# Slot filling behind the first pair's weights, and fewer waits in TensorE's program for sorted tiles

## Chip, cores and metric

The kernel runs on one core of a Trainium2 chip, as one launch. The metric is the time of that launch on the device in microseconds (us), the median of several runs. The core has five engines that run programs of their own and meet at semaphores: TensorE (PE; the profile lists its matmuls as PE and its weight loads as PEld), VectorE (DVE), ScalarE (ACT), GpSimd (POOL) and SyncE (SP). Of each engine the instructions that only wait, load a register or issue a DMA are shown as its own queue (PEq or PEldq, DVEq, SPq and so on) and don't count as busy.

## The reference

Input x is 16 sequences of 256 tokens, 128 wide, in float32: 4096 tokens. Eight sublayers follow one another, each added to x behind a layer norm. A lookahead attention with 16 heads, a mixture of 8 experts of which the best 2 serve each token, a latent attention, and the same mixture again make layer 0; a helical attention, a mixture of which the best 1 serves each token, a recurrent (delta) attention, and that mixture again make layer 1.

```python
x = x + attn_a0(layernorm(x), W_qkv, W_out)        # aa
x = x + top2(layernorm(x), Wg, bg, W1, b1, ...)    # fa
x = x + attn_b0(layernorm(x), ...)                 # ab
x = x + top2(layernorm(x), Wg, bg, W1, b1, ...)    # fb
x = x + attn_a1(layernorm(x), ...)                 # helical
x = x + top1(layernorm(x), gate_w, ...)            # fc
x = x + attn_b1(layernorm(x), ...)                 # delta
x = x + top1(layernorm(x), gate_w, ...)            # fd
# top2, of one token x and its two experts e with weights w_e:
#   y = x + sum_e w_e * (relu(x @ W1[e] + b1[e]) @ W2[e] + b2[e]), then a layer norm with gamma and beta
# top1, of one token and its expert: shared(x) + (silu(x' @ gate[e].T) * (x' @ up[e].T)) @ down[e].T,
#   with x' = x * sigmoid(largest logit)
```

## The kernel before

The stages run one behind the other, each between barriers of all engines. x, its normed form and constants stay in SBUF. The two parts that the change touches are these.

**The start of the lookahead attention** (stage aa, from L264). It takes 8 pairs of heads, and for each the 16 sequences, 128 steps. SP's program (L303 to L316) begins with four DMAs that have nothing to do with attention: they fill four DRAM buffers, into which the mixtures will sort their tokens, from a tile of zeros and default addresses in SBUF (`rt_empty`, made by POOL in the stage before at L155 and L160): two `rt_pairs` (L306) and two `rt_slots` (L308). Behind them comes a loop over the pairs, its first turn written out with the integer 0 (`turns`, L57): wait until the pair before was projected (L312; `reached` leaves a wait for 0 out, L34), ask for the pair's weights `aa_w` (L313), wait, ask for its output weights (L315). At the end (L316) SP waits for all four fillings. POOL copies each step's input (L335), PE projects it (`project`, L363 and L367; L360 waits for the weights), ACT keeps the projections (L471), and the other engines follow. A layer norm (L242, L260) runs ahead of the stage.

**The sorted tiles of the four mixtures.** A mixture sends every token's row by an indirect DMA to a slot, so that the tokens of one expert lie in whole tiles of 128 slots; slots that are left over keep the filling. Then it loads the slots in parts, each with its own semaphore `arrived[i]`, and works through the tiles, whose expert is read from a small table `owner`. In `top2_mixture` (fa and fb, L842) there are 71 tiles, in parts that begin at tiles 0, 4 and 20; in `routed_mixture` (fc and fd, L1185) 39, in parts that begin at 0, 4 and 16. Each tile j takes these steps; all buffers between engines are double, `yout` fourfold:

- PE turns the tile (`turn_x`, L994; L1314), ACT keeps it as `xT` (`keep_x`).
- PE projects it with its expert's weights (`up`, L1000; `both`, L1318 to L1323). The expert's number is first read into a register (`value_load`, L997; L1317).
- In fa and fb DVE adds the bias (L1135), giving `hid` and `bias_ok`. In fc and fd ACT makes a tanh, and DVE two steps (L1468 and L1472), giving `hid` and `rhid_ok`.
- PE turns `hid` (`turn_h`, L1007; L1330), ACT keeps it as `hidT` (L1061: relu; L1383) and signals `h_ok`.
- PE projects it down (`lower`, L1016; L1339), DVE writes `yout` (`keep_y`, L1142; L1479) once the return of four tiles before has landed and signals `y_ok`; POOL returns it by an indirect DMA to the tokens' rows (L941; L1261). At the start of a part POOL first converts the part's addresses (`home`, L937).

PE's program is unrolled and skewed; a turn n holds

```python
turn_x(n); turn_h(n - 3); lower(n - 4); up(n - 1)      # both(n - 1) in fc and fd
```

and each of these steps waits with two `wait_ge`: for its input, and (through `reached`) for the reader of the buffer that it writes again, two tiles back. Of two waits in front of one instruction the compiler attaches one to the instruction and issues the other as an instruction of its own, which the trace lists as EVENT_SEMAPHORE at L37, the line of `reached`.

Of the kernel before, what the change touches and what calls it, by code (L numbers as in the profile page):

```python
# [18 lines left out]
P = 128  # L19
# [14 lines left out]
def reached(eng, sem, count):  # L34

    if not isinstance(count, int) or count > 0:
        eng.wait_ge(sem, count)  # L37
# [19 lines left out]
def turns(eng, count):  # L57

    yield 0
    with eng.Fori(1, count) as i:  # L60
        yield i
# [202 lines left out]
def lookahead_attention(nc, sh, rt, empty, W_qkv, W_out):  # L264
# [8 lines left out]
    with Phase(nc, "aa") as ph:  # L273
        emptied = ph.sem("emptied")
# [27 lines left out]
        with nc.Block() as block:  # L302
            @block.sync  # L303
            def _(sp):
                for slots in rt.slots2:
                    sp.dma_start(slots.rearrange("(j p) c -> p j c", p=P), empty[:]).then_inc(emptied, 16)  # L306
                for slots in rt.slots:
                    sp.dma_start(slots.rearrange("(j p) c -> p j c", p=P), empty[:, 0:rt.tiles, 0:rt.ROW]  # L308
                                 ).then_inc(emptied, 16)
                for p in turns(sp, PAIRS):  # L310

                    reached(sp, projected, 3 * BATCH * p)  # L312
                    sp.dma_start(w[:], w_dram[:, :, bass.ds(p * P, P)]).then_inc(w_in, 16)  # L313
                    reached(sp, y_mm, BATCH * p)
                    sp.dma_start(wo[:], W_out[bass.ds(p * P, P), :]).then_inc(wo_in, 16)  # L315
                sp.wait_ge(emptied, 64)  # L316

            @block.gpsimd
# [523 lines left out]
def top2_mixture(nc, sh, rt, slots, name, Wg, bg, W1, b1, W2, b2, gamma, beta):  # L842
# [8 lines left out]
    PARTS = ((0, 4), (4, 20), (20, ROUTED))  # L851
    with Phase(nc, name) as ph:
# [31 lines left out]
        arrived = [ph.sem(f"arrived{i}") for i in range(len(PARTS))]  # L884
# [7 lines left out]
        def part_of(j):  # L892
            return next(i for i, (lo, hi) in enumerate(PARTS) if lo <= j < hi)

        with nc.Block() as block:
# [55 lines left out]
            def _(pe):  # L951
# [37 lines left out]
                owners = {}  # L989

                def turn_x(j):
                    pe.wait_ge(arrived[part_of(j)], 16)
                    reached(pe, x_ok, j - 1)
                    nc.tensor.transpose(ps_t[:, j % 2, 0:P], xin[:, j, 2:P + 2], sh.ident[:]).then_inc(x_mm, 1)  # L994

                def up(j):
                    owners[j] = nc.tensor.value_load(owner[0:1, j:j + 1], min_val=0, max_val=E - 1)  # L997
                    pe.wait_ge(x_ok, j + 1)
                    reached(pe, bias_ok, j - 1)
                    nc.tensor.matmul(ps_up[:, j % 2, 0:F], xT[:, j % 2, :],  # L1000
                                     w1[:, bass.ds(owners[j], 1), :].rearrange("p a c -> p (a c)"),
                                     start=True, stop=True).then_inc(up_mm, 1)

                def turn_h(j):
                    pe.wait_ge(bias_ok, j + 1)
                    reached(pe, h_ok, j - 1)
                    for i in range(2):  # L1007
                        ins = nc.tensor.transpose(ps_h[:, j % 2, i * P:(i + 1) * P], hid[:, j % 2, i * P:(i + 1) * P],
                                                  sh.ident[:])
                    ins.then_inc(h_mm, 1)  # L1010
# [14 lines left out]
                for n in range(ROUTED + 4):  # L1025
                    if n < ROUTED:
                        turn_x(n)
                    if 0 <= n - 3 < ROUTED:
                        turn_h(n - 3)
                    if 0 <= n - 4 < ROUTED:  # L1030
                        lower(n - 4)
                    if 0 <= n - 1 < ROUTED:
                        up(n - 1)
# [151 lines left out]
def routed_mixture(nc, sh, ew, rt, slots, name, gate_w):  # L1185
# [9 lines left out]
    PARTS = ((0, 4), (4, 16), (16, ROUTED))  # L1195
    with Phase(nc, name) as ph:
# [27 lines left out]
        arrived = [ph.sem(f"arrived{i}") for i in range(len(PARTS))]  # L1224
        fetched = [ph.sem(f"fetched{i}") for i in range(4)]

        def part_of(j):
            return next(i for i, (lo, hi) in enumerate(PARTS) if lo <= j < hi)

        with nc.Block() as block:  # L1230
# [35 lines left out]
            def _(pe):  # L1266
# [42 lines left out]
                owners = {}  # L1309

                def turn_x(j):
                    pe.wait_ge(arrived[part_of(j)], 16)
                    reached(pe, x_ok, j - 1)
                    nc.tensor.transpose(ps_t[:, j % 2, 0:P], xin[:, j, 1:P + 1], sh.ident[:]).then_inc(x_mm, 1)  # L1314

                def both(j):
                    owners[j] = nc.tensor.value_load(owner[0:1, j:j + 1], min_val=0, max_val=E - 1)  # L1317
                    pe.wait_ge(x_ok, j + 1)  # L1318
                    reached(pe, rhid_ok, j - 1)
                    nc.tensor.matmul(ps_g[:, j % 2, 0:F], xT[:, j % 2, :],  # L1320
                                     ew.gate[:, bass.ds(2 * owners[j], 2), :].rearrange("p a c -> p (a c)"),
                                     start=True, stop=True)
                    nc.tensor.matmul(ps_g[:, j % 2, F:2 * F], xT[:, j % 2, :],  # L1323
                                     ew.up[:, bass.ds(2 * owners[j], 2), :].rearrange("p a c -> p (a c)"),
                                     start=True, stop=True).then_inc(both_mm, 1)

                def turn_h(j):
                    pe.wait_ge(rhid_ok, j + 1)
                    reached(pe, h_ok, j - 1)
                    for i in range(2):  # L1330
                        ins = nc.tensor.transpose(ps_u[:, j % 2, i * P:(i + 1) * P], hid[:, j % 2, 0, i * P:(i + 1) * P],  # L1331
                                                  sh.ident[:])
                    ins.then_inc(h_mm, 1)
# [14 lines left out]
                for n in range(ROUTED + 4):  # L1348
                    if n < ROUTED:
                        turn_x(n)  # L1350
                    if 0 <= n - 3 < ROUTED:
                        turn_h(n - 3)
                    if 0 <= n - 4 < ROUTED:
                        lower(n - 4)
                    if 0 <= n - 1 < ROUTED:
                        both(n - 1)
# [1017 lines left out]
```

## Time and profile before

| | |
|---|---|
| median of 3 runs | 4413.18 us (4410.03 to 4414.11) |
| profiled execution | 4403.01 us, of which the span of instructions 4401.3 us |
| PE busy | 3398.4 us (77%), its weight loads 2798.6 us (64%) |
| DVE busy | 2698.6 us (61%) |
| ACT busy | 1907.2 us (43%) |
| POOL busy | 1609.0 us (37%) |
| mean granted clock of PE | 0.881 |

The median is the number that a change is compared with; the profiled execution is one run whose every instruction was recorded, and the durations of single steps come from it. Shares of busy time are means over stages with different limits, so they say little of a single stage. The core's 16 DMA engines move 96.03 MB in all.

### The profile page before, as it was taken

How to read it: one execution, taken by the hardware profiler on the slowest of the kernel's cores; microseconds unless marked ns; L12 is line 12 of the kernel's file. 1: busy time of each engine (PE TensorE's matmuls, PEld its weight loads, DVE VectorE, ACT ScalarE, POOL GpSimd, SP SyncE). 2: the span in 40 equal slices, each digit the busy share in tenths (PEclk: the TensorE clock that was granted, in tenths of full speed). 3: DMA queues.
4: the chain of work that ended last, by engine and by line, in shares of the span. 5: the costliest groups of instructions: out<-in, count | busy, mean ns of one | idle time of the engine just before them, and what ended most of it. 6: DMA issues, size and time to landing. Idle time of an engine off the chain costs nothing. (4 is left out here: it accounts for less than half of the span.)

```text
span 4401.3 us, 91493 instructions
## 1 busy us (share of the span) xinstructions
PE 3398.4 (77%) x23484; PEld 2798.6 (64%) x23484; DVE 2698.6 (61%) x8449; ACT 1907.2 (43%) x5752; POOL 1609.0 (37%) x2825
## 2 busy tenths in 40 slices
PE   0999999999994649999983838999999685433176
PEld 0888888888883536777763616888888563322155
DVE  2566666666663365666661444777777255999954
ACT  0555555555551215555541324666666233211122
POOL 1222222222223734444435622333333051666633
PEclk6999999999995869999995969999999697766578
DMA  9000000000001220000002210000000121000003
GB/s 154 3 4 4 0 4 4 4 1 4 4 0 53 86 58 8 2 4 3 2 3 65 84 49 5 6 6 6 6 6 6 33 59 29 1 1 1 1 18 88
DMA packets 137483, 96.03 MB, mean 22 GB/s; under 512 B 21552, under 2 KB 127296, under 8 KB 137088
## 3 DMA queue, kind: packets, MB, share of 16 engines
q1 hardware_dynamic: 124160, 67.30, 6.9%
q0 software_dynamic: 13184, 27.19, 1.8%
q8 instruction: 49, 0.80, 0.1%
q14 instruction: 90, 0.74, 0.1%
HBM read 45.86 MB, written 43.87 MB: 20 GB/s over the span
## 5 line engine op out<-in xcount | busy, mean ns | idle before, releaser
L340 POOL TENSOR_TENSOR aa_prob<-aa_prob,aa_inv 128x128 f32<-128x128 f32 (+1 forms) x512 | 249.2, 508 | 991.5 <-DVE aa_inv L556 991.5
L363 PE MATMUL aa_proj<-aa_xs,aa_w 128*128 128x256 f32 x1280 | 362.3, 398 | 86.4 <-DMA aa_w<-in_L_attn_a_W_qkv 85.0
L471 ACT ACTIVATE aa_qkv<-aa_proj 128x512 f32<-128x512 f32 x384 | 229.4, 597 | 331.4 <-PE aa_proj L363 270.7
L650 POOL TENSOR_TENSOR ab_prob<-ab_prob,ab_inv 128x128 f32<-128x128 f32 (+1 forms) x512 | 248.8, 507 | 334.2 <-DVE ab_inv L805 327.5
L773 ACT ACTIVATE ab_prob<-ab_ps_score,ab_low 128x128 f32<-128x128 f32 (+1 forms) x512 | 211.7, 424 | 303.5 <-PE ab_ps_turn L707 301.5
L1845 ACT ACTIVATE lm_prob<-lm_ps_score,lm_low 128x256 f32<-128x256 f32 x512 | 237.7, 470 | 234.8 <-DVE lm_low L1914 160.5
L1790 PEld LDWEIGHTS lm_ps_out<-la_v,lm_probT 128*128 128x128 f32 x2048 | 253.3, 191 | 72.4 <-issue 66.1
L1732 POOL TENSOR_TENSOR lm_sq<-lm_comp 128x512 f32<-128x512 f32 x128 | 133.7, 1044 | 441.2 <-DVE lm_comp L1887 441.2
L363 PEld LDWEIGHTS aa_proj<-aa_xs,aa_w 128*128 128x128 f32 x1280 | 213.8, 191 | 118.8 <-issue 86.5
L529 DVE SCALAR_TENSOR_TENSOR aa_look<-aa_th_look,aa_ahead 128x384 f32<-128x384 f32 x256 | 183.2, 716 | 161.9 <-ACT aa_th_look L477 161.9
L2174 PE MATMUL dr_bank<-da_rT,da_spread 128*128 (+1 forms) x256 | 95.8, 462 | 240.6 <-ACT dr_RW L2192 232.9
L1769 PE MATMUL lm_ps_score<-lm_unit 128*128 128x256 f32 x1024 | 270.5, 387 | 5.5 <-DVE lm_unit L1904 5.5
L1790 PE MATMUL lm_ps_out<-la_v,lm_probT 128*128 (+1 forms) x2048 | 257.2, 252 | 19.0 <-issue 13.3
L2224 POOL TENSOR_TENSOR dr_toward<-dr_S,XN 128x64 f32<-128x64 f32 x512 | 180.8, 372 | 212.8 <-DVE dr_S L2253 150.5
L260 PE MATMUL n_turned<-ident,XN 128*128 128x128 f32 x256 | 55.6, 370 | 234.3 <-DVE XN L242 234.1
L799 DVE TENSOR_REDUCE ab_low<-ab_ps_score 128x1 f32<-128x128 f32 (+1 forms) x512 | 147.1, 349 | 141.3 <-PE ab_ps_score L700 141.3
L1914 DVE TENSOR_REDUCE lm_low<-lm_ps_score 128x2 f32<-128x512 f32 x256 | 176.4, 689 | 92.9 <-PE lm_ps_score L1769 90.9
L482 ACT ACTIVATE aa_th_su<-aa_look_su 128x384 f32<-128x384 f32 x256 | 125.7, 491 | 242.8 <-PE aa_look_su L407 242.8
L488 ACT ACTIVATE aa_prob<-aa_minus,aa_low 128x128 f32<-128x128 f32 (+1 forms) x512 | 225.4, 444 | 0.9 <-DVE aa_low L548 0.9
L2174 PEld LDWEIGHTS dr_bank<-da_rT,da_spread 128*128 128x128 f32 x256 | 58.7, 236 | 255.6 <-issue 245.9
L536 DVE SCALAR_TENSOR_TENSOR aa_gated<-aa_th_su,aa_look_su 128x384 f32<-128x384 f32 x256 | 141.8, 554 | 108.3 <-ACT aa_th_su L482 106.7
L1904 DVE TENSOR_TENSOR lm_unit<-lm_comp,lm_inv_n 64x512 f32<-64x512 f32 x256 | 201.4, 787 | 1.9 <-ACT lm_inv_n L1834 0.2
(507 smaller groups left out, 9960.3 us busy)
## 6 DMA issues: line engine op xcount, KB each, us to landing
rt_pairs<-rt_empty SPq DMA_DIRECT2D x2, 4615.0 KB, 36.4
rt_slots<-rt_empty SPq DMA_DIRECT2D x2, 2515.5 KB, 39.7
fa_xin<-rt_back SPq DMA_DIRECT2D x8, 512.0 KB, 7.3
fb_xin<-rt_back SPq DMA_DIRECT2D x8, 512.0 KB, 7.3
lm_unit<-la_qk SPq DMA_DIRECT2D x256, 16.0 KB
XN<-rt_back SPq DMA_DIRECT2D x8, 512.0 KB, 5.7
fa_xin<-rt_pairs SPq DMA_DIRECT2D x1, 3315.0 KB
fb_xin<-rt_pairs SPq DMA_DIRECT2D x1, 3315.0 KB
```

The lines of the kernel that those rows point to most:

```text
L340: ins = nc.gpsimd.tensor_tensor(prob[:, h, a:b], prob[:, h, a:b], inv[:, h, t:t + 1].broadcast_to([P, b - a]), ALU.mult)
L363: ins = nc.tensor.matmul(proj[:, i * SEQ:(i + 1) * SEQ], w[:, m, :], xs[:, k, :], start=True, stop=True)
L471: nc.scalar.activation(qkv[:, k, j, :, :].rearrange("p a b -> p (a b)"), proj[:], ACT.Copy, scale=SCALE if j == 0 else 1.0).then_inc(kept, 1)
L488: nc.scalar.activation(prob[:, h, a:b], minus[:, h, a:b], ACT.Exp, bias=low[:, h, t:t + 1], scale=-1.0, accum_out=total[:, h, t:t + 1]).th ...
L529: nc.vector.scalar_tensor_tensor(out=look[:, h, :], in0=th_look[:, h, :], scalar=1.0, in1=ahead[:], op0=ALU.add, op1=ALU.mult).then_inc(lo ...
L650: ins = nc.gpsimd.tensor_tensor(prob[:, h, a:b], prob[:, h, a:b], inv[:, h, t:t + 1].broadcast_to([P, b - a]), ALU.mult)
L773: nc.scalar.activation(prob[:, h, a:b], ps_score[:, h, a:b], ACT.Exp, bias=low[:, h, t:t + 1], accum_out=total[:, h, t:t + 1]).then_inc(ex ...
L1769: ins = nc.tensor.matmul(ps_score[:, h, c * SEQ:(c + 1) * SEQ], unit[:, j, i, h, 0, c, :], unit[:, j, i, h, 1, :, :], start=True, stop=True)
L1790: ins = nc.tensor.matmul(ps_out[:, i, (2 * h + s) * HD:(2 * h + s + 1) * HD], probT[:, h, t, s * P:(s + 1) * P], v[:, bass.ds((n % BATCH) ...
L1845: nc.scalar.activation(prob[:, h, s, :], ps_score[:, h, s * SEQ:(s + 1) * SEQ], ACT.Exp, bias=low[:, h, s:s + 1], accum_out=totals[:, i, h ...
L1904: ins = nc.vector.tensor_tensor(unit[rows, j, i, h], comp[rows, j, i], inv_n[rows, j, i].unsqueeze(2).broadcast_to([64, 2, 2, HALF]), ALU. ...
L2224: nc.gpsimd.tensor_tensor(toward[:, :, part], S[:, :, part], WV[:, half, :, part, j], ALU.add).then_inc(toward_ok, 1)
```

## The change

In the first turn of SP's loop the four fillings are issued behind the request for the pair's weights and its output weights, no longer in front of them. In the sorted tiles of all four mixtures PE's program loses waits: `turn_x` waits for `arrived` in the first tile of a part alone, and the `reached` waits of `turn_x`, `up` (or `both`) and `turn_h` are gone. Each of the events that they waited for is implied by another wait that PE's program has already passed: `up(n - 1)` waits for `x_ok` of tile n - 1, so `turn_x(n + 1)` needn't; `turn_h(j - 2)` stands in front of `up(j)` and waits for `bias_ok` (or `rhid_ok`) of tile j - 2; `lower(j - 2)` stands in front of `turn_h(j)` and waits for `h_ok`. The waits of `lower` are kept. Nothing else changes.

```diff
--- before.py
+++ after.py
@@ -302,17 +302,18 @@
         with nc.Block() as block:
             @block.sync
             def _(sp):
-                for slots in rt.slots2:
-                    sp.dma_start(slots.rearrange("(j p) c -> p j c", p=P), empty[:]).then_inc(emptied, 16)
-                for slots in rt.slots:
-                    sp.dma_start(slots.rearrange("(j p) c -> p j c", p=P), empty[:, 0:rt.tiles, 0:rt.ROW]
-                                 ).then_inc(emptied, 16)
                 for p in turns(sp, PAIRS):
 
                     reached(sp, projected, 3 * BATCH * p)
                     sp.dma_start(w[:], w_dram[:, :, bass.ds(p * P, P)]).then_inc(w_in, 16)
                     reached(sp, y_mm, BATCH * p)
                     sp.dma_start(wo[:], W_out[bass.ds(p * P, P), :]).then_inc(wo_in, 16)
+                    if isinstance(p, int):
+                        for slots in rt.slots2:
+                            sp.dma_start(slots.rearrange("(j p) c -> p j c", p=P), empty[:]).then_inc(emptied, 16)
+                        for slots in rt.slots:
+                            sp.dma_start(slots.rearrange("(j p) c -> p j c", p=P), empty[:, 0:rt.tiles, 0:rt.ROW]
+                                         ).then_inc(emptied, 16)
                 sp.wait_ge(emptied, 64)
 
             @block.gpsimd
@@ -989,21 +990,19 @@
                 owners = {}
 
                 def turn_x(j):
-                    pe.wait_ge(arrived[part_of(j)], 16)
-                    reached(pe, x_ok, j - 1)
+                    if j == PARTS[part_of(j)][0]:
+                        pe.wait_ge(arrived[part_of(j)], 16)
                     nc.tensor.transpose(ps_t[:, j % 2, 0:P], xin[:, j, 2:P + 2], sh.ident[:]).then_inc(x_mm, 1)
 
                 def up(j):
                     owners[j] = nc.tensor.value_load(owner[0:1, j:j + 1], min_val=0, max_val=E - 1)
                     pe.wait_ge(x_ok, j + 1)
-                    reached(pe, bias_ok, j - 1)
                     nc.tensor.matmul(ps_up[:, j % 2, 0:F], xT[:, j % 2, :],
                                      w1[:, bass.ds(owners[j], 1), :].rearrange("p a c -> p (a c)"),
                                      start=True, stop=True).then_inc(up_mm, 1)
 
                 def turn_h(j):
                     pe.wait_ge(bias_ok, j + 1)
-                    reached(pe, h_ok, j - 1)
                     for i in range(2):
                         ins = nc.tensor.transpose(ps_h[:, j % 2, i * P:(i + 1) * P], hid[:, j % 2, i * P:(i + 1) * P],
                                                   sh.ident[:])
@@ -1309,14 +1308,13 @@
                 owners = {}
 
                 def turn_x(j):
-                    pe.wait_ge(arrived[part_of(j)], 16)
-                    reached(pe, x_ok, j - 1)
+                    if j == PARTS[part_of(j)][0]:
+                        pe.wait_ge(arrived[part_of(j)], 16)
                     nc.tensor.transpose(ps_t[:, j % 2, 0:P], xin[:, j, 1:P + 1], sh.ident[:]).then_inc(x_mm, 1)
 
                 def both(j):
                     owners[j] = nc.tensor.value_load(owner[0:1, j:j + 1], min_val=0, max_val=E - 1)
                     pe.wait_ge(x_ok, j + 1)
-                    reached(pe, rhid_ok, j - 1)
                     nc.tensor.matmul(ps_g[:, j % 2, 0:F], xT[:, j % 2, :],
                                      ew.gate[:, bass.ds(2 * owners[j], 2), :].rearrange("p a c -> p (a c)"),
                                      start=True, stop=True)
@@ -1326,7 +1324,6 @@
 
                 def turn_h(j):
                     pe.wait_ge(rhid_ok, j + 1)
-                    reached(pe, h_ok, j - 1)
                     for i in range(2):
                         ins = nc.tensor.transpose(ps_u[:, j % 2, i * P:(i + 1) * P], hid[:, j % 2, 0, i * P:(i + 1) * P],
                                                   sh.ident[:])
```

## Rows read from the trace of the kernel before

**Rows 1.** Windows: length, PE, PEld, DVE, ACT, POOL busy, clock, DMA share, GB/s

```profile
0.00:110.00 110.00, 6.84 (x32) 4.65 (x32) 25.62 (x75) 6.30 (x10) 15.12 (x32) 0.67 0.91 154
110.00:1320.00 1210.00, 1182.80 (x9194) 1017.19 (x9194) 792.50 (x2555) 710.57 (x2046) 290.58 (x636) 0.99 0.01 3
```

**Rows 2.** List of waits, 0 to 140 us: who <- whom: total, times, longest

```profile
PE aa_proj L363 <- DMA aa_w<-in_L_attn_a_W_qkv: 78.7, 1, 78.7
```

**Rows 3.** Timeline, 0 to 140 us: start, duration, instruction [idle before <- for what]

```profile
35.08 18.18 SPq L306 DMA_DIRECT2D rt_pairs<-rt_empty  x2
...
91.08 13.89 SPq L313 DMA_DIRECT2D aa_w<-in_L_attn_a_W_qkv  x1
...
112.44 2.05 PE L363 MATMUL aa_proj<-aa_xs,aa_w 128*128 128x256 f32 x4 [78.69 <-DMA aa_w<-in_L_attn_a_W_qkv]
```

**Rows 4.** Timeline of sorted tiles in fa, around 1484 and 1511 us

```profile
1484.87 0.97 POOL L941 DMA_INDIRECT rt_back<-fa_yout,fa_home  x1 [0.30 <-issue]
...
1511.29 0.30 PEld L1000 LDWEIGHTS fa_ps_up<-fa_w,fa_xT 128*128 128x128 f32 x2 [0.22 <-issue]
...
1512.35 0.38 ACT L1061 ACTIVATE fa_hidT<-fa_ps_h 128x256 f32<-128x256 f32 x1
...
1512.77 0.30 PEld L1000 LDWEIGHTS fa_ps_up<-fa_w,fa_xT 128*128 128x128 f32 x2 [0.20 <-issue]
```

**Rows 5.** PE's queue by line: count: ns min/median/max, first to last start

```profile
L37 PEldq EVENT_SEMAPHORE  x3: 51/51/51, 1511.3 to 1511.6; - x3
...
L997 PEldq SEQ_ASSERT  x1: 18/18/18, 1512.5 to 1512.5; - x1
...
L1000 PEldq FUSED_REGOPS  x1: 46/46/46, 1512.7 to 1512.7; - x1
...
L997 PEldq SEQ_ASSERT  x1: 18/18/18, 2432.9 to 2432.9; - x1
...
L1000 PEldq FUSED_REGOPS  x1: 52/52/52, 2433.0 to 2433.0; - x1
...
L37 PEldq EVENT_SEMAPHORE  x1: 51/51/51, 3602.2 to 3602.2; - x1
```

**Rows 6.** Timeline of fc around 3600 us and fd around 4307 us

```profile
3599.71 0.69 PE L1320 MATMUL fc_ps_g<-gateT,fc_xT 128*128 x2
...
3601.75 0.42 DVE L1472 SCALAR_TENSOR_TENSOR fc_hid<-fc_gu,fc_ps_g 128x256 f32<-128x256 f32 x1
...
3603.42 0.30 PEld L1320 LDWEIGHTS fc_ps_g<-gateT,fc_xT 128*128 128x128 f32 x2
...
4306.66 0.30 PEld L1320 LDWEIGHTS fd_ps_g<-gateT,fd_xT 128*128 128x128 f32 x2 [0.43 <-issue]
...
4308.30 0.30 PEld L1320 LDWEIGHTS fd_ps_g<-gateT,fd_xT 128*128 128x128 f32 x2
```

**Rows 7.** Timeline, 256 to 268 us: the second pair's weights

```profile
258.31 0.61 SPq L313 DMA_DIRECT2D aa_w<-in_L_attn_a_W_qkv  x1
...
262.23 1.13 PE L363 MATMUL aa_proj<-aa_xs,aa_w 128*128 128x256 f32 x4 [1.14 <-DMA aa_w<-in_L_attn_a_W_qkv]
```

**Rows 8.** Short windows, columns as in rows 1

```profile
38.00:40.00 2.00, 0.00 (x0) 0.00 (x0) 0.00 (x0) 0.00 (x0) 0.06 (x1) 0.50 1.14 266
112.00:120.00 8.00, 6.19 (x16) 4.01 (x16) 0.00 (x0) 1.20 (x2) 0.00 (x0) 0.50 0.00 0
1472.00:1480.00 8.00, 7.83 (x50) 6.26 (x49) 3.51 (x10) 3.53 (x12) 4.82 (x7) 1.00 1.20 303
```

**Rows 9.** By line, 1472 to 1480 us: count | busy, mean ns | idle

```profile
L1061 ACT ACTIVATE fa_hidT<-fa_ps_h 128x256 f32<-128x256 f32 x6 | 2.3, 384 | 0.0
```

**Rows 10.** POOL's returns by line, in fa (from tile 4) and fb

```profile
L941 POOL DMA_INDIRECT rt_back<-fa_yout,fa_home x66: 966/969/985, 1481.0 to 1578.2; - x66
...
DMA to landing us min/median/max: 2.3/2.3/3.2
...
L941 POOL DMA_INDIRECT rt_back<-fb_yout,fb_home x71: 966/969/1001, 2438.4 to 2544.4; - x71
```

## The prediction

> **What bounds the kernel now.** I began with the busy times by stretch, the page's slices and then windows: TensorE (PE) is busy for 1182.8 of the 1210 us from 110 to 1320, but for 6.8 of the first 110 [rows 1]. The change touches that stretch and the four sorted mixtures, so each was then read by itself.
>
> In the first 140 us the list of waits has one entry that matters: the projection waits 78.7 us for the DMA that brings its weights [rows 2]. The timeline says why. The stage opens at 35.08 with SyncE (SP) issuing the four slot fillings; the instruction that asks for the weights comes up only at 91.08, takes 13.89 us to issue behind them, and the first matmul starts at 112.44 [rows 3]. Nothing computes meanwhile, and the fillings have no reader before the first mixture, beyond 1350 us.
>
> In the sorted tiles PE looks full, but its weight loads show an idle piece in front of the first projection of every tile, put down to "issue" [rows 4]: nothing the profile shows was waited for. The cause is found by asking for the lines of PE's own queue, whose instructions are not counted as busy. Per tile it loads the owner, works out addresses, asserts, and executes four stand-alone waits, before it can issue [rows 5]. The steps of PE from tile to tile (1511.29 to 1512.77, 1.48 us [rows 4]) are the length of that list. The other two mixtures (fc, fd) are read from [rows 6]: there steps of two lengths alternate, which points to a loop over two tiles.
>
> **Part 1, the fillings behind the first weights.** Moved past are four DMA issues, all on SP's queue; GpSimd's (POOL) queue holds no DMA in this stage. The weights are then asked for at 35.08. How long they take alone is shown by the second pair: asked for at 258.31, its first matmul waits for them until 262.23, 3.92 us [rows 7]. So the first matmul comes at 39.00 instead of 112.44: **73.4 us**. In 38 to 40 the granted clock is at its lower level, as it is in 112 to 120 [rows 8], so the cold start of the stage is only moved, not saved.
>
> What the fillings now run beside: issue 56.0 us (35.08 to 91.08) and data until just before 112.44, some 76 us, so from about 37 to 114, next to the first ten steps of attention. Behind them on SP stands the second pair's request, now at 258.31 and then at about 185, with 70 us to spare; the stage's closing wait for them lies over a thousand us later. Does the traffic slow the engines? The nearest stretch is 1472 to 1480, where slots are loaded at 303 GB/s while all engines work [rows 8]: the ReLU activation takes 384 ns on the mean there [rows 9] and 0.38 us at 1512.35, when little moves [rows 4]. That is loading into SBUF and not reading from it, so it is only near. I take nothing; as far bound, a tenth of 76 us, 7.6 us lost. If the weights' packets were served in turn with the fillings' and not ahead of them, 3.92 us would at most double. Bounds of this part: 73.4 down to 73.4 - 7.6 - 3.9 = 61.9; better than 73.4 is excluded by the same 3.92 us.
>
> **Part 2, the waits of the 71-tile mixtures (fa, fb).** Three of four stand-alone waits per tile go; the attached wait for the arrival goes without an instruction of its own. A wait executes in 51 ns, but costs its dispatch too. With one between them, the assert and the address arithmetic start at 1512.5 and 1512.7; in the second tile of fb, where that wait does not exist yet, at 2432.9 and 2433.0 [rows 5]. Three waits with a turn in between start within 0.3 us, 1511.3 to 1511.6 [rows 5]. So 0.1 us each, between 0.05 (execution alone) and 0.12; three are 0.3, and PE's list falls from 1.48 to about 1.18 us a tile.
>
> It will not be followed that far, for another is late next: POOL, which returns each tile. Back to back a return takes 1.27 us, 0.97 busy and 0.30 of its own issue ahead of it (the one at 1484.87 [rows 4]), while from the fifth tile 65 steps take 97.2 us (1481.0 to 1578.2), 1.495 each [rows 10]. The forecast is that POOL sets the step: 66 steps x (1.495 - 1.27) = 14.9, less some 0.5 for the index cast of the third part, which is hidden now, and 0.3 for the first tiles: 14.1. The first four tiles keep their times, since their returns wait behind the slot loads. The second pass (71 returns, 2438.4 to 2544.4 [rows 10]) has the same pace: **28.2 us** for both. Bounds: with 0.05 us a wait, 0.15 x 132 = 19.8; not more than 29.8, all of POOL's slack.
>
> **Part 3, the waits of the 39-tile mixtures (fc, fd).** Same three waits, but the list is not what binds. One tile's first projection starts at 3599.71, its hidden layer ends on VectorE (DVE) at 3601.75 + 0.42 = 3602.17, PE's queue executes its next stand-alone wait at 3602.2 [rows 5], and the projection two tiles on is loaded at 3603.42 [rows 6]. So PE's queue stands at the turning of the hidden layer, whose weight load carries the wait for DVE, until DVE is done, and the loop of 3.71 us over two tiles is: 2.46 to the hidden layer and 1.25 of queue. Of the removed waits only the one before the projection lies in the 1.25; the other two are executed while the queue would stand anyway, and their cover is that standing. Gain 0.1 per two tiles, 0.05 x 76 = **3.8 us** for both; bounds 0 and, were the loop gone, PE's shortest step of 1.64 (4306.66 to 4308.30 [rows 6]) against 1.855: 0.215 x 76 = 16.3.
>
> For this the Trainium skill has a rule that says otherwise (Perfetto Trace Analysis, section Tensor Engine Instruction): a matrix instruction with a semaphore wait is pushed into a wait queue and the sequencer goes on to the next instruction. By the rule in the Trainium skill the queue would not stand, this part would be at its upper bound of 16.3 instead of 3.8, and the sum 117.9. The record at 3602.2, just behind DVE's end, speaks against it.
>
> **The sum.** 73.4 + 28.2 + 3.8 = 105.4. The profiled execution took 4403.0 us (span 4401.3), 10 us under the median of the runs, 4413.2; the difference is carried to the median: 4413.2 - 105.4 = **4307.8** (4297.6 by the profiled execution's own time).
>
> **Rivals.**
> *PE does not stand at attached waits.* If PE's queue goes on past a weight load whose wait is still open, the loop over two tiles is gone: fc and fd fall to 1.64 a tile, 16.3 instead of 3.8, time 4295.3. For it: some steps already take 1.64. Against it: the alternation and the place of the stand-alone wait [rows 5, 6]. 6%. (This is what the rule of the Trainium skill, Perfetto Trace Analysis, would make of these stages.)
>
> *The tiles stay where they are.* DVE keeps a tile's output only when the return of four tiles before has landed. Landing takes 2.3 us [rows 10]; with steps of 1.27, four take 5.1, which leaves over a microsecond. If returns landed as late as they do under the slot loads, or another loop held PE, parts 2 and 3 would give nothing: 4413.2 - 73.4 = 4339.8. 6%.
>
> *The fillings press on the attention stage.* The 7.6 and 3.9 us above are lost: 4319.3. For it: it is 76 us of 16 busy DMA engines reading the memory that the engines read. Against it: the means of [rows 9]. 11%.
>
> *Slower than before.* Place: the second pair's weights, behind the fillings on SP's queue. If the fillings, now beside work, ran on past 185, PE would stand for each microsecond more, as it does today. To give back all 105.4 they would have to end near 290 rather than 114, three times as long; at the 7.6 us allowed above they are far from it. At four times, some 340, the time would be 4413 + 50 = 4463. 1%.
>
> The forecast itself holds the other 76%.
>
> **How the numbers follow.** Low end: all upper bounds, 73.4 + 29.8 + 16.3 = 119.5, 4293.7, taken as 4294, which holds the first rival. High end: all lower bounds, 61.9 + 19.8 + 0 = 81.7, 4331.5, taken as 4331, which holds the third. Left out are the second and fourth rivals and a rest. A measurement of this kernel can tell about 0.2% (8.8 us) from no change. Every case but the fourth gains over 70 us: faster 0.98, same 0.01, slower 0.01.
>
> **What would show it right or wrong.** Right: the first matmul of the projection near 39 us; a wait for the weights near 5 us in place of 78.7; the fillings' data beside attention until about 114, and the second pair's weights unharmed; in fa and fb, POOL's returns 1.27 us apart through most of the pass, their idle time put down to "issue" and no longer to DVE; PE's stand-alone waits down from four to one a tile; in fc and fd, pairs of steps that sum to some 3.6 us, with the one stand-alone wait still right behind DVE's hidden layer. Wrong: attention steps longer before 114 than after (then the third rival), returns still 1.5 apart with PE idle (the second), or fc at 1.64 (the first).

## The result, and the profile after

The changed kernel takes **4297.98 us** in the median of 4 runs (4294.72 to 4310.06) against 4411.99 before (4 runs): 114.0 us less, a ratio of 0.9746 with a 95% interval of 0.9726 to 0.9767. Forecast were 4307.8 us and a gain of 105.4, with 4294 to 4331 as the range. Run again beside the experiments below, it took 4296.67 us (5 runs) against 4406.64 (9 runs), 0.9761 [0.9745, 0.9776]: 110.0 us less. The recorded execution took 4310.06 us (span 4308.3), 92.9 under the recorded one of before. That the same change shows 93, 110 and 114 us is itself a part of what had to be explained.

**The start of the attention.** The timeline of the changed kernel from 30 to 140 us (start, duration, instruction, idle before it) answers to [rows 3]:

```profile
35.08 0.61 SPq L308 DMA_DIRECT2D aa_w<-in_L_attn_a_W_qkv  x1
...
36.42 23.50 SPq L313 DMA_DIRECT2D rt_pairs<-rt_empty  x2
...
39.54 2.05 PE L364 MATMUL aa_proj<-aa_xs,aa_w 128*128 128x256 f32 x4 [5.79 <-DMA aa_w<-in_L_attn_a_W_qkv]
...
59.96 45.25 SPq L315 DMA_DIRECT2D rt_slots<-rt_empty  x2
```

The weights are asked for first, and the projection starts at 39.54 instead of 112.44; the wait is 5.79 us where it was 78.69. SP needs 69 us to issue the fillings (56 before), beside a working attention.

**The sorted tiles.** POOL's returns from the fifth tile on, of fa and then of fb (count: ns min/median/max, first to last start; below each, what ended the idle time ahead of them, in us and times), answer to [rows 10]:

```profile
L942 POOL DMA_INDIRECT rt_back<-fa_yout,fa_home x67: 964/971/982, 1409.0 to 1497.5; - x67
...
  DVE fa_yout L1141: 18.9, 43
  issue: 7.0, 23
...
L942 POOL DMA_INDIRECT rt_back<-fb_yout,fb_home x67: 964/969/985, 2365.1 to 2452.9; - x67
...
  DVE fb_yout L1141: 16.7, 38
  issue: 8.5, 28
```

66 steps take 88.5 us in fa and 87.8 in fb, 1.34 and 1.33 each, where they took 1.495. The forecast was 1.27. And in 43 of 67 cases in fa, 38 in fb, POOL still waits for DVE: it isn't the one that sets the step.

In fc one tile of the changed kernel reads, in the timeline (and, the third row, in the lines of PE's own queue, as in [rows 5]):

```profile
3512.35 0.42 DVE L1469 SCALAR_TENSOR_TENSOR fc_hid<-fc_gu,fc_ps_g 128x256 f32<-128x256 f32 x1
...
3513.98 0.30 PEld L1318 LDWEIGHTS fc_ps_g<-gateT,fc_xT 128*128 128x128 f32 x2 [0.17 <-issue]
...
L37 PEldq EVENT_SEMAPHORE  x1: 51/51/51, 3512.8 to 3512.8; - x1
```

The hidden layer ends at 3512.77, PE's queue executes its next stand-alone wait at 3512.8, and the projection is loaded at 3513.98: 1.21 us behind the hidden layer, where [rows 6] give 1.25. Over the tiles 6 to 34 the mean fell from 1.263 to 1.180 (0.083), the median from 1.258 to 1.161 (0.097) and the least from 1.254 to 1.149 (0.105). A stand-alone wait in this list takes 0.051 us and the pause that comes with it 0.055, so the least shows the whole of one wait; in some tiles a longer pause elsewhere in the list takes a part back.

By stage (from the first to the last instruction that writes one of the stage's own tiles; the sixth line from the helical stage's last matmul to the first transpose of the expert weights; us):

| | before | changed | changed, again |
|---|---|---|---|
| attention aa | 1292.4 | 1219.3 | 1219.0 |
| fa | 258.9 | 250.2 | 247.2 |
| fb | 259.8 | 248.7 | 247.7 |
| fc | 155.6 | 153.0 | 153.1 |
| fd | 155.3 | 154.0 | 153.9 |
| projection behind the helical attention | 37.0 | 39.2 | 30.3 |
| span | 4401.3 | 4308.3 | 4291.3 |

The first five lines give 96.9 and 101.0 us. The sixth has nothing to do with the change, and differs by 9 us between two recordings of one program.

### The profile page after: what moved, and what is told of

Its sections match the earlier page's. It is cut to its first block and busy times, and to the rows that moved or that the text cites. A ratio compares the mean times of both kernels' runs of the same rounds, so it can differ in the third digit from the quotient of the medians.

```text
span 4308.3 us, 90857 instructions
## 1 busy us (share of the span) xinstructions
PE 3387.3 (79%) x23484; PEld 2803.7 (65%) x23484; DVE 2698.0 (63%) x8449; ACT 1907.7 (44%) x5752; POOL 1608.3 (37%) x2825
## 5 line engine op out<-in xcount | busy, mean ns | idle before, releaser
L1787 PEld LDWEIGHTS lm_ps_out<-la_v,lm_probT 128*128 128x128 f32 x2048 | 254.0, 192 | 72.6 <-issue 66.1
L1911 DVE TENSOR_REDUCE lm_low<-lm_ps_score 128x2 f32<-128x512 f32 x256 | 176.6, 690 | 92.3 <-PE lm_ps_score L1766 90.3
```

The source lines that it names most:

```text
L1787: ins = nc.tensor.matmul(ps_out[:, i, (2 * h + s) * HD:(2 * h + s + 1) * HD], probT[:, h, t, s * P:(s + 1) * P], v[:, bass.ds((n % BATCH) ...
```

## The experiments

**1. The fillings alone.** The first hunk of the change, and nothing of the others.

> Part 1 alone: the slot fillings issued behind the first pair's weights, every wait of the sorted tiles kept. Theory: the attention stage (first to last instruction 1292.4 us before, 1219.3 in the changed kernel) takes 1219 to 1220, the sorted stages keep their lengths of before (first to last projection of the tiles: fa 106.7, fb 107.7, fc 71.5, fd 72.5), and the whole is 73 us faster than the kernel before, some 4338 us. Rival (the fillings press on the attention, and the changed kernel's waits hid that): attention over 1225 us. Rival (the fillings only move the loss): total within 20 us of before.

It took 4328.09 us, the kernel before beside it 4414.84. In the timeline of this kernel:

```profile
39.01 2.04 PE L364 MATMUL aa_proj<-aa_xs,aa_w 128*128 128x256 f32 x4 [5.29 <-DMA aa_w<-in_L_attn_a_W_qkv]
```

The attention took 1218.3 us. From its first projection to its end it takes 1214.3 us here, 1214.9 in the changed kernel and 1215.1 in the kernel before, so the fillings cost the work beside them nothing that can be seen. The sorted stages kept their lengths only roughly: from first to last projection fa and fb took 109.4 and 109.3 us, 2.6 and 1.5 more than in the recording of before, with the same code; fc took 71.6 and fd 71.5. The median step from projection to projection in fa and fb is 1.51 us as before, and the longer steps lie around the tenth tile; sums over a whole stage can differ by this much without any change. Between the recordings the gain is 74.9 us (4401.3 and 4326.4), against the run beside it 87, larger than 73; the next two experiments say why it can be.

**2. The waits alone.** All hunks but the first.

> Parts 2 and 3 alone: waits left out in all four mixtures, the fillings in front of the first weights as before. Theory: the attention stage takes 1292 us as before; from first to last projection fa 97.7, fb 96.6, fc 70.1, fd 70.4 us as in the changed kernel, each within 1 us; the whole 20 to 25 us faster than before. Rival (the two parts help each other, since the difference of the medians, 114 us, is more than 73 + 24): fa and fb shorter still than in the changed kernel, or the whole more than 30 us faster.

It took 4377.81 us, 37.0 less than before. The sorted stages were as in the changed kernel (97.4, 95.5, 70.0 and 70.1 us from first to last projection), but the attention took 1303.3 us and not 1292:

```profile
123.44 2.05 PE L363 MATMUL aa_proj<-aa_xs,aa_w 128*128 128x256 f32 x4 [89.72 <-DMA aa_w<-in_L_attn_a_W_qkv]
```

The first projection came 11 us later than in [rows 3], with the same instructions ahead of it. So the price of the fillings in front is no constant. Against the recording of before the four sorted stages together took 28.3 us less and the projection behind the helical attention 6.6 (30.4 against 37.0), the attention 10.9 more: 24.0 of the 25.3 us between the spans (4401.3 and 4376.0). The run of the kernel before beside this one was 37.0 us slower, over the 30 that the rival named; that would follow if its first projection, too, came near 123, but it was not recorded. Parts 1 and 2 don't help each other: fa and fb are no shorter than in the changed kernel by more than its own two recordings differ.

**3. The kernel before, recorded again.**

> The kernel before, recorded once more, for the spread. In its first recorded execution the first projection started at 112.4 us and the whole took 4403.0, 10 us under the median; in the run with the waits alone it started at 123.4. Theory: what differs between executions of the kernel before is how long the fillings take, so that the first projection starts between 112 and 124 us here, the attention stage from there to its end takes 1215 us as in every run so far, and an execution of 4411 to 4415 us goes with a start near 122. Rival (the spread lies elsewhere, in PE's clock in the later stages): a start near 112 and a total above 4410, or the reverse.

```profile
114.57 2.05 PE L363 MATMUL aa_proj<-aa_xs,aa_w 128*128 128x256 f32 x4 [80.83 <-DMA aa_w<-in_L_attn_a_W_qkv]
```

4404.26 us, with a first projection at 114.57 and 1215.4 us from there to the attention's end. Three recordings with the fillings in front thus give 112.4, 114.6 and 123.4; those without, here and below, 38.8 to 39.7. Neither recording of the kernel before was one of 4411 to 4415 us, so that those go with a start near 122 stays unproven.

The record names the chip of each of these runs, and the length of the fillings goes with it. Experiments 1, 2, 5 and 6 ran on one chip: in each of their four recordings 115 to 165 GB/s still move between 118 and 122 us. This one and experiments 4 and 7 ran on a second, experiment 8 on a third: there it is at most 4 GB/s. The kernel before took 4414.84 us (one run) on the first, and in the median of nine runs 4406.64 on the second and 4399.83 on the third. So a part of what the fillings cost depends on the chip, as far as these recordings show; for the runs of the result the chip is not on record.

**4. Half of the fillings in front.** The changed kernel, with

```diff
+                for slots in rt.slots2:
+                    sp.dma_start(slots.rearrange("(j p) c -> p j c", p=P), empty[:]).then_inc(emptied, 16)
                 for p in turns(sp, PAIRS):
...
                     if isinstance(p, int):
-                        for slots in rt.slots2:
-                            sp.dma_start(slots.rearrange("(j p) c -> p j c", p=P), empty[:]).then_inc(emptied, 16)
                         for slots in rt.slots:
```

> The changed kernel with two of the four fillings (rt_pairs, 9.23 of 14.26 MB, 18 us of issue) put back in front of the first weights, the other two left behind them. Theory: the weights' packets stand behind the fillings' data, which moves at about 190 GB/s, so the first projection starts at 35 + 49 + 4 = 88 us, between 80 and 95. Rival (only SP's issue of the fillings counts, 18 to 24 us, and the data runs beside): at 57 to 63 us. The whole is later than the changed kernel by the same amount, since nothing else depends on it.

```profile
35.05 19.45 SPq L306 DMA_DIRECT2D rt_pairs<-rt_empty  x2
54.54 25.82 SPq L310 DMA_DIRECT2D aa_w<-in_L_attn_a_W_qkv  x1
...
87.78 2.05 PE L364 MATMUL aa_proj<-aa_xs,aa_w 128*128 128x256 f32 x4 [54.06 <-DMA aa_w<-in_L_attn_a_W_qkv]
```

The first projection starts at 87.78, forecast 88. So it is the data of the fillings that the weights stand behind, and not only their issue: SP is free for the weights at 54.5, and the instruction itself then takes 25.8 us to issue where it takes 0.6 with nothing in front. The whole took 4337.71 us, 41 more than the changed kernel's median beside it (4296.67), where 49 were expected; the attention alone is 47.9 us longer than in that kernel's recording (1266.9 and 1219.0), the span 44.6.

**5. The waits split by stage.** fa and fc lose only the wait in front of the projection, fb and fd only the others. The edit of `top2_mixture` (that of `routed_mixture` is the same with fc, `both` and `rhid_ok`):

```diff
+                alone = name == "fa"
...
-                    if j == PARTS[part_of(j)][0]:
+                    if alone or j == PARTS[part_of(j)][0]:
                         pe.wait_ge(arrived[part_of(j)], 16)
+                    if alone:
+                        reached(pe, x_ok, j - 1)
...
                     pe.wait_ge(x_ok, j + 1)
+                    if not alone:
+                        reached(pe, bias_ok, j - 1)
...
                     pe.wait_ge(bias_ok, j + 1)
+                    if alone:
+                        reached(pe, h_ok, j - 1)
```

> The changed kernel with its waits split by stage: fa and fc lose only the wait in front of the projection (up, both); fb and fd lose only the others (turn_x's two and turn_h's). Theory of the prediction: in fa and fb the length of PE's list binds, so each wait that goes is worth 0.1 us a tile: fa's middle steps 1.38 to 1.41, fb's 1.28 to 1.33. In fc and fd PE's queue stands at the turning of the hidden layer, so only the wait in front of the projection counts: fc 70.0 us from first to last projection as in the changed kernel, fd 72.5 as before. Rival (every executed wait counts alike): fc about 70.9, fd about 71.1. Rival (PE's queue never stands, a full gain was blocked by something else): fc and fd both as in the changed kernel.

The weight loads of the projections (two a tile; count: ns, first to last start) of this kernel:

```profile
L1330 PEld LDWEIGHTS fc_ps_g<-gateT,fc_xT x78: 186/189/337, 3495.1 to 3566.1; 128*128 128x128 f32 x78
L1330 PEld LDWEIGHTS fd_ps_g<-gateT,fd_xT x78: 186/189/337, 4218.4 to 4290.7; 128*128 128x128 f32 x78
L1005 PEld LDWEIGHTS fa_ps_up<-fa_w,fa_xT x142: 186/189/338, 1394.5 to 1497.2; 128*128 128x128 f32 x142
L1005 PEld LDWEIGHTS fb_ps_up<-fb_w,fb_xT x142: 186/189/338, 2357.6 to 2456.7; 128*128 128x128 f32 x142
```

By the same rows fa and fb take 106.8 and 107.8 us in the kernel before and 97.9 and 96.6 in the changed one (95.5 and 95.8 recorded again), fc and fd 71.6 and 72.6 before (71.6 and 71.5 in experiment 1) and 70.1 and 70.4 changed.

In fa and fb the stalls at the start of the parts blur these sums; the median step from one projection to the next leaves them out. It is 1.51 us in the kernel before, 1.42 with one wait gone (fa; 1.38 to 1.41 were expected), 1.37 with two (fb; 1.28 to 1.33 expected), and 1.31 and 1.32 with all three. So each wait was worth less than 0.1 us, and both stages missed their range. For fb the loop of the next experiment gives a reason: the wait that stays there stands in it, and 1.32 with a third of 0.105 is 1.36, an estimate; it was not tested by itself.

In fd (72.3) the two waits gave nothing that stands out of 71.5 to 72.6, where the rival that every wait counts alike had 71.1: they are executed while the queue stands. In fc the one wait gave 0.6 of 1.5 us, and its 71.0 is nearer to that rival's 70.9 than to the 70.0 expected; fd is what speaks against the rival. The trace shows where a part of the rest stayed: over the tiles 6 to 34 the pause in PE's queue in front of the address arithmetic of `lower`, behind the hidden layer, is 0.12 us in the median here and 0.08 in the changed kernel. What makes it is not settled.

**6. Owner loads ahead of a wait.** In the changed kernel the number of the tile's expert is loaded one place earlier: in fa on DVE in front of `keep_y`, in fb and fc on PE in front of `turn_h`; fd is left as it is. On PE (`owner_of` holds the `value_load` that stood in `up` and `both`):

```diff
                     if n < ROUTED:
                         turn_x(n)
+                    if name in ('fb', 'fc') and 0 <= n - 1 < ROUTED:
+                        owner_of(n - 1)
                     if 0 <= n - 3 < ROUTED:
                         turn_h(n - 3)
```

It tests what sets the 1.33 us. In the changed kernel's timeline of fa one loop over three tiles reads:

```profile
1443.42 0.30 PEld L1000 LDWEIGHTS fa_ps_up<-fa_w,fa_xT 128*128 128x128 f32 x2
...
1444.28 0.61 PE L1015 MATMUL fa_ps_y<-fa_w,fa_hidT 128*128 x4
...
1444.93 0.35 DVE L1141 TENSOR_SCALAR fa_yout<-fa_ps_y,fa_xin 128x128 f32<-128x128 f32 x1
...
1445.76 0.42 DVE L1134 TENSOR_TENSOR fa_hid<-fa_ps_up,fa_b1b 128x256 f32<-128x256 f32 x1 [0.48 <-PE fa_ps_h L1007]
...
1447.39 0.30 PEld L1000 LDWEIGHTS fa_ps_up<-fa_w,fa_xT 128*128 128x128 f32 x2
```

and in the lines of DVE's and PE's own queues, between them:

```profile
L1131 DVEq TENSOR_LOAD <-fa_owner x1: 306/306/306, 1444.9 to 1444.9; - x1
...
L37 PEldq EVENT_SEMAPHORE  x1: 51/51/51, 1446.2 to 1446.2; - x1
```

Behind the projection of 1443.42 PE comes to the next `lower`, which ends at 1444.89; `keep_y` follows at 1444.93; only with it does DVE's queue come to the owner load of the next bias, so the bias starts 0.83 us behind it, though its input is ready at 1445.43; it ends at 1446.19, PE's queue goes on at 1446.2 with its own owner load, and the next projection but two is loaded at 1447.39. 3.97 us over three tiles are 1.32 a tile.

> The changed kernel with an owner load moved ahead of a wait: in fa on DVE (ahead of keep_y), in fb and fc on PE (ahead of turn_h), fd untouched. Theory: the steps of 1.31 us that are left in fa and fb are a loop over three tiles: lower ends, keep_y starts, DVE's list (0.83 us to the bias), bias 0.43, PE's list (1.15 us to the projection), PE's own work 1.47 to the end of the next lower: 3.95 over three tiles. Shortening either list by 0.65 us takes the loop to 1.10, and POOL's 1.27 binds in fa and in fb alike: first to last projection 95 us in both (97.7 and 96.6 in the changed kernel), middle returns all at 1.27 to 1.29. In fc the loop over two tiles falls from 3.6 to 2.95 us, PE's own work of 1.63 a tile binds: 63 us instead of 70.1; fd stays at 70.4. Rival (POOL and late returns make the 1.31): fa and fb unchanged. Rival (PE's queue goes on past an attached wait): fc unchanged at 70.

The returns of this kernel in fa (DVE's load ahead) and fb (PE's), from the fifth tile on, and the projections of fc and fd:

```profile
L942 POOL DMA_INDIRECT rt_back<-fa_yout,fa_home x67: 963/967/982, 1408.4 to 1493.0; - x67
...
L942 POOL DMA_INDIRECT rt_back<-fb_yout,fb_home x67: 963/968/982, 2359.0 to 2443.2; - x67
...
L1337 PEld LDWEIGHTS fc_ps_g<-gateT,fc_xT x78: 190/192/337, 3476.7 to 3540.1; 128*128 128x128 f32 x78
L1337 PEld LDWEIGHTS fd_ps_g<-gateT,fd_xT x78: 186/189/338, 4190.6 to 4260.8; 128*128 128x128 f32 x78
```

66 steps take 84.6 and 84.2 us, 1.28 each, whichever of the two lists is shortened: now POOL's 1.27 binds, and "issue" ended its idle time 47 times of 67 in fa and 39 times in fb. fc fell to 63.4 us, every step but the first three and the last 1.64, the shortest that PE's own work had shown in [rows 6]; fd, untouched, stayed at 70.2. The passes themselves came to 91.9 and 90.9 us from first to last projection, 3 to 4 us under the expectation of 95, in part because that went by POOL's pace and forgot that PE may be further ahead of POOL at the end: in fb the last return starts 6.0 us behind the last projection, in the changed kernel 4.6.

**7. The loads ahead in all four mixtures,** on PE alone, and the changed kernel once more beside it.

> The changed kernel with PE's owner load put ahead of turn_h in all four mixtures. From the run that had it in fb and fc: fa and fb 91 us from first to last projection (97.7 and 96.6), POOL's returns 1.27 us apart throughout; fc and fd 63.3 us (70.1 and 70.4), every step 1.64. Together 26 us under the changed kernel, some 4270 us. Rival (the gain of one stage is lost at the next, by PE's clock): less than 15 us.

> The changed kernel, again, beside the others on one chip. If the fillings of the kernel before take 10 us longer in most executions than in the one recorded first, the difference of the medians is 105 + 10 = 115 us within 5; if the 114 us were chance, it comes out near 105 or below, with 93, the difference of the two recorded executions, as the rival's number.

4283.43 us (5 runs; 0.9725 [0.9711, 0.9738] of before), the changed kernel 4296.67: 13 us less, not 26, and under the 15 of the rival. The sorted stages reached the lengths expected (91.9 and 92.3 us from first to last projection in fa and fb, 63.4 and 63.1 in fc and fd), but the gain was 20.0 us: fa, fb, fc and fd together took 782.0 us, and the changed kernel, whose fa and fb came out shorter this time, 802.0. Of these 20.0, 8.7 were lost where no line had been touched, in the projection behind the helical attention. The changed kernel's 110.0 us under the kernel before lie at the very edge of the 115 within 5, so that expectation is neither borne out nor refuted. Windows there (length; PE, PEld, DVE, ACT, POOL busy; granted clock; DMA share, GB/s), first of the changed kernel as first recorded, then recorded again, then of this kernel:

```profile
3340.00:3348.00 8.00, 6.10 (x26) 5.05 (x24) 1.50 (x3) 1.68 (x3) 5.38 (x5) 0.50 0.00 0
```

```profile
3327.00:3333.00 6.00, 4.02 (x16) 3.24 (x16) 0.69 (x1) 1.13 (x2) 5.29 (x5) 0.50 0.01 3
3333.00:3341.00 8.00, 5.82 (x45) 5.10 (x46) 2.06 (x3) 1.86 (x4) 4.56 (x4) 1.00 0.00 0
```

```profile
3331.00:3339.00 8.00, 6.13 (x25) 5.33 (x26) 1.37 (x2) 1.64 (x3) 4.96 (x5) 0.50 0.00 0
```

The granted clock falls to 0.50 (1.2 GHz) as this piece begins. In the second recording it is back at 1.00 after some 6 us, and PE does 45 matmuls in 8 us; in the others it stays down, and PE does 26 and 25. From the helical stage's last matmul to the first transpose of the expert weights the three take 39.2, 30.3 and 39.0 us. The kernel before lies between (37.0 and 36.9).

The nine runs of the changed kernel agree with this, though only two were recorded instruction by instruction: the mean granted clock of the three that took 4307 us and more is 0.885 to 0.886, of the six others (4290.91 to 4301.0) 0.888 to 0.890. And in the ten recordings with this code in the piece its length goes with the moment at which the clock falls: 30.2 to 30.4 us where it falls 0.3 to 0.8 us ahead of the end of the helical stage's last matmul (three), 36.9 to 37.1 where it falls 0.6 behind it (three), 39.0 to 39.3 where it falls more than a microsecond ahead of it or behind it (four). That is a pattern in ten recordings; no run sets the moment by itself.

**8. The same, with PE fed in that piece:** it turns the next chunk before it projects this one (the matmuls left out here are those of before, with c - 1 in the second group).

```diff
-                for c in range(CH):
-                    reached(pe, kept, c - 1)
...
-                    pe.wait_ge(kept, c + 1)
-                    reached(pe, added, c - 1)
...
+                for c in range(CH + 1):
+                    if c < CH:
+                        reached(pe, kept, c - 1)
...
+                    if c > 0:
+                        pe.wait_ge(kept, c)
+                        reached(pe, added, c - 2)
...
```

> The kernel with the owner loads ahead, and in the output projection behind the helical attention (lo) PE turns the next chunk before it projects this one, so that it no longer stands idle while ACT copies. In the recordings so far the stretch from the helical stage's end to the expert weights' first transpose took 30.2 to 30.4 us where PE's granted clock there rose (0.88 to 0.89), 36.9 to 37.1 at 0.59 and 39.0 to 39.3 where it stayed at 0.50, with the same code. Theory: this stretch is a part of the spread and of the gain that the owner loads missed (best gained 20 us in the sorted stages against the changed kernel beside it and lost 8.7 here). With PE fed, the stretch takes 22 to 26 us if the clock rises and about 30 if it stays at 0.50, so 9 to 17 us less than 39.0, and the whole is some 4270 us. Rival (what is lost at the clock there is lost elsewhere when this part is shorter): the stretch falls, but the whole stays above 4280.

```profile
3335.00:3343.00 8.00, 8.00 (x72) 7.83 (x71) 4.13 (x6) 3.15 (x6) 5.33 (x5) 1.00 0.00 0
```

4270.22 us (5 runs) against 4399.83 before, 0.9706 [0.9693, 0.9719]. The piece takes 22.7 us, the clock is up within its first 6 us, and all five runs lie within 4.5 us of each other, where the changed kernel's five spread over 17 and those of experiment 7 over 8. Between the recordings of experiments 7 and 8 the piece is 16.4 us shorter and the span 13.2. Of the versions tried this has the lowest time, but it ran on another chip than experiment 7: against the kernel before beside each it gained 129.6 us, experiment 7 gained 123.2, and the two intervals overlap.

## Why the prediction was right, and where only by size

**Part 1: right, and the mechanism shown.** 73.4 us were forecast and 73.1 seen between the recordings, with a first projection at 39.54 (forecast 39.00). The third rival, pressure on the attention, is out: 1214 to 1215 us from the first projection on, with the fillings beside it or not. The fillings ran on to about 125 us in the first recording, and to about 115 in the second, near the 114 forecast; the second pair's weights, asked for at 185.4, had them long behind: the slower rival's place was never in danger. What the prediction did not see is that the term is no constant: 112 to 123 us for the first projection with the fillings in front, so 73 to 84 us of gain. That better than 73.4 was excluded held for the recorded execution alone.

**Part 2: right in the kind, too large in the size, and the step that failed is "POOL sets the step".** Three waits at 0.1 us each are what PE's list lost (0.051 and a pause of 0.055 each), and POOL's 1.27 us is a true bound, reached in experiment 6. But above both the list of 1.18 and POOL's 1.27 lay a loop that the prediction had not looked for: `keep_y`, DVE's owner load, the bias, PE's owner load, 1.32 a tile. That this loop set the step is shown by experiment 6, where shortening either of its two lists brought the step down to POOL's. With steps of 1.33 to 1.34 and some stalls at the parts the two stages gave 19.9 us in the first recording and 23.8 in the second, against 28.2 with 19.8 as the lower bound. The sentence "another is late next" was right; the choice of the next one was made from the row that was easiest to price.

**Part 3: right.** 3.8 forecast, 3.9 and 3.8 measured in the stages. That it comes out so close is in part luck: from first to last projection fd took 71.5 to 72.6 us in the three recordings with all waits, so its share lies between 1 and 2.4 us; in fc, 71.6 in all three, it is 1.4 to 1.5. That PE's queue stands at the turning of the hidden layer is shown three times over: its next own instruction comes 0.05 us behind DVE's end over the tiles 6 to 34 (in the median), before and after; the two waits executed under its standing gave nothing in fd; and the owner load, put in front of the place where it stands, took the mean step of these tiles from 1.82 to 1.64. So the first rival is out, and with it what a rule would have made of these stages. The Trainium skill (Perfetto Trace Analysis, section Tensor Engine Instruction) has the sequencer go on once a waiting instruction is pushed into a wait queue. Here it did not come to its own next instruction, which stands behind the two weight loads and two matmuls of `turn_h`, before the wait of the first of these loads was over, and the measurement decides. How far it went within these four is not shown.

**The sum.** In the recordings parts 1 to 3 gave 96.9 and 101.0 us where 105.4 was forecast. Terms outside the sum moved the whole: the clock in the projection behind the helical attention (39.2 us in the first recording, 30.3 in the second, 37.0 before) and the kernel before itself, whose medians of 4406.64 and 4411.99 us are 4 and 9 us above its recorded execution. Between the recordings this adds up: 101.0, 6.7 of that projection and 2.3 elsewhere are the 110.0 between the spans of 4401.3 and 4291.3. For the medians the spread of the fillings in front is the likely cause, but no execution of the kernel before near 4412 us was recorded. The predicted median of 4307.8 missed by 9.8 us, on the slow side, while its parts were too large by 8.5 and 4.4. Carrying the 10 us between recording and median over to the new kernel did not hold: its median lies 12 us under its first recording and 4 above its second. Without them the forecast was 4297.6, which the median of 4297.98 meets by luck: what the parts lacked, the terms outside the sum made up.

## What to carry to other kernels

A DMA that nobody needs soon still holds up all that is issued behind it on its queue, by the time of its data and not of its issue: put the small urgent load first. Whether the fillings would have spared the load from another engine's queue was not tried. Where an engine's own queue is the limit, count what stands in it between the instruction that blocks and the one that is late; register loads (about 0.6 us here: 0.30 for the load, 0.15 and 0.02 for what is done with the number, and the pauses between them) are worth more than waits (0.1 us), and moving them in front of the blocking wait cost nothing that could be seen here. When a bound is removed, close every loop that passes through the shortened list before naming the next bound, a loop over three tiles as well as one over one or two.

## What was not expected of the hardware

The granted clock in one short piece with an idle PE differed from recording to recording of one program, and took 9 us with it: 26 or 45 matmuls in the same 8 us. In the one recording in which PE was given work in its gaps the clock rose early (72 matmuls in 8 us at 1.00), and its five runs lay closest together; that the clock rose in the four others too is inferred from that. And the instruction that asks for 0.4 MB of weights, 0.6 us to issue on an idle queue, took 13.9 to 15.3 us behind 14 MB and 25.8 us behind 9 MB: SP itself was held by what lay ahead.
